# Eight of image 0's lines: depthwise taps moved from VectorE to ScalarE and GpSimd, inside a codebook search

## The chip, the cores and the metric

One core of a Trainium2 chip runs the whole program. The metric is the time of one execution on the device, in microseconds, as the median of several runs. The engines are TensorE (matmuls, into PSUM), VectorE, ScalarE, GpSimd and SyncE; each has its own instruction stream and works through it strictly in order, and they meet only at semaphores. GpSimd also issues the indirect DMAs, the gathers, from its own stream.

## The reference, cut to what matters

Four layers on an input of 2 images of 128 channels and 48 x 48 pixels, each on a group-normed input and added to the running x:

```python
x = x + _L0_conv_ref(_gn(x), ...)     # softmax-weighted dilated branches, 1x1 conv, batch norm
x = x + _L1_conv_ref(_gn(x), codebook)  # nearest of 8192 code vectors for every pixel
x = x + _L2_conv_ref(_gn(x), Wk, bk)    # depthwise 3x3, its weights made from the image
x = x + _L3_conv_ref(_gn(x), ...)     # two deformable 3x3 convolutions with group norms

def _L1_conv_ref(z, codebook):          # per pixel z_flat: argmin over codes
    d = jnp.sum(z_flat ** 2, axis=1, keepdims=True) + jnp.sum(codebook ** 2, axis=1) - 2.0 * jnp.matmul(z_flat, codebook.T)
    idx = jnp.argmin(d, axis=1)
    z_q = codebook[idx].reshape(B, H, W, C)

def _L2_conv_ref(x, Wk, bk):            # nine weights for each channel of each image
    pooled = x.mean(axis=(2, 3))
    kern = jax.nn.relu(pooled @ Wk.T + bk)
    out = lax.conv_general_dilated(xr, kern, ..., feature_group_count=b * c)
```

The change is in the third of them, for image 0.

## The kernel before, in words

Channels lie on the 128 partitions, the 2 x 2304 pixels along the free dimension. The codebook search goes over the pixels in nine blocks of 512 (n = 0 to 8), and for each block over the codebook in four steps (s = 0 to 3) of 16 units (k = 0 to 15). A unit is three bfloat16 matmuls on TensorE (lines 1490 to 1492), which give the scores of 128 blocks of codes for 512 pixels in one of five PSUM buffers, and one running maximum: ScalarE takes units 0 and 1 (line 1667), VectorE scans the other fourteen (line 1962). The maxima are turned by TensorE (line 1379) and copied by ScalarE (line 1601). Then the best block of codes of each pixel is found exactly: for each of the four groups of 128 pixels in a block (u = 0 to 3) VectorE finds the best entry (lines 1777, 1782), GpSimd gathers its eight code vectors (line 2093), multiplies them by the pixel (line 2105), ScalarE sums (line 1592), VectorE chooses among the eight (lines 1788, 1792), GpSimd makes the number of the code (line 2113) and fetches that code's row (line 2118). TensorE turns the four rows (line 1399), VectorE subtracts the pixel from them (line 1807), and GpSimd adds the result to x (lines 2125, 2127). All orders are written out by hand: tables such as `UPPER_AT` say behind which unit an extra piece stands.

Image 0 ends within the fifth block, so its next layer, the depthwise convolution, is done beside the search of the seventh block (n = 6, called L0 in the code). Of image 0's 48 lines VectorE does the upper 24, one instruction per tap on 128 x 1152 elements, that is, multiply by the tap's weight and add into x (`upper_tap`, line 262). TensorE does the lower 24 in three pieces of eight lines, nine diagonal matmuls each (`pe_lower_tap`, line 276), which VectorE adds to x (line 283). At the block's last unit VectorE takes the turned codes, subtracts, and then computes the statistics of all of image 0 (line 139) for the norm ahead of the last layer; the eighth block's scans stand behind this. GpSimd's part of the block's last two steps, in `step` of its program, is: fetch 0, product 3, fetch 1 (s = 2), then fetch 2 and fetch 3 (s = 3), then the add into x. TensorE's turn of the codes stands at the end of step 3 and waits for all four fetches; the eighth block's matmuls are behind it. After the search the four rounds of the deformable convolution follow, for which GpSimd issues some 640 gathers (line 2202).

Of the kernel before, what the change touches and what calls it, by code (L numbers as in the profile page):

```python
# [16 lines left out]
B, H, W = 2, 48, 48  # L17
HW = H * W
N = B * HW
WP = W + 2  # L20
# [4 lines left out]
ROWS = 8  # L25
CH = ROWS * W
NCH = H // ROWS
# [4 lines left out]
TAPS = 9  # L32
# [11 lines left out]
ALU = mybir.AluOpType  # L44
ACT = mybir.ActivationFunctionType
# [147 lines left out]
class Depthwise:  # L193
# [5 lines left out]
    def __init__(self, tools, ctx, a, x, xpad, gm32):  # L199
        self.a, self.x, self.xpad, self.gm32 = a, x, xpad, gm32  # L200
        self.wk = tools.sb(ctx, "wk", [P, TAPS, P])
        self.bk = tools.sb(ctx, "bk", [P, TAPS])
        self.kern = tools.sb(ctx, "kern", [P, TAPS])
        self.pooled = tools.sb(ctx, "pooled", [P, 1])
        self.norm = ImageNorm(tools, ctx)
        self.loaded = tools.sem(ctx, "wk_loaded")
        self.pooled_ready = tools.sem(ctx, "pooled_ready")
        self.kern_ready = tools.sem(ctx, "kern_ready")
        self.applied = tools.sem(ctx, "applied")
        self.done = [tools.sem(ctx, "tap_done") for _ in range(B)]  # L210
        self.kern_done = tools.sem(ctx, "kernels_done")
        self.diag_ready = tools.sem(ctx, "diagonals_ready")
        self.lower_ready = tools.sem(ctx, "lower_taps_ready")
        self.lower_added = tools.sem(ctx, "lower_taps_added")

    def sp(self, sp):
        sp.dma_start(self.wk[:], self.a["wk"]).then_inc(self.loaded, 16)
# [31 lines left out]
    def dve_kernels(self, dve, b, ps):  # L249
# [3 lines left out]
        dve.sem_inc(self.kern_done, 1)  # L253
        dve.wait_ge(self.applied, b + 1)

    def upper_tap(self, dve, k):
        v = self.xpad[:, 0:PADDED].rearrange("p (r w) -> p r w", w=WP)
        v = v[:, k // 3:k // 3 + H // 2, k % 3:k % 3 + W]
        xb = self.x[:, 0, 0:HW // 2].rearrange("p (r w) -> p r w", w=W)
        if k:  # L260
            dve.wait_ge(self.done[0], k)
        dve.scalar_tensor_tensor(xb, v, self.kern[:, k:k + 1], xb, ALU.mult, ALU.add).then_inc(self.done[0], 1)
# [795 lines left out]
def carve(region, sizes):  # L1058

    at, out = 0, []  # L1060
    for n in sizes:
        out.append(region[:, at:at + n])
        at += n
    return out
# [12 lines left out]
def finale(nc, tools, a, code_rows, x, xpad, ident, gm32, gm8, nc2, depthwise, between, places, out):  # L1077
# [42 lines left out]
    L0 = EARLY + 1  # L1120
# [15 lines left out]
    with ExitStack() as ctx:  # L1136
        y0 = tools.sb(ctx, "y_first", [P, HW])
        m0, m1, runs = carve(region_max, [PXT * GROUPS * P] * 2 + [4 * PX])
        maxima = [m.rearrange("p (u g) -> p u g", u=PXT) for m in (m0, m1)]
        r = carve(runs, [PX] * 4)  # L1140
# [79 lines left out]
        off_lead = lead_ps[:, 0:CH]  # L1220
        lower_ps = [off_lead, z_ps.rearrange("p u c -> p (u c)")[:, 0:CH], off_lead]
        diag = region_early[:, PX * EARLY:PX * EARLY + TAPS * P]
        off_ps = [score[0][:, 0:CH]] + [z_ps.rearrange("p u c -> p (u c)")[:, PX - CH:PX]] * (JOBS - 1)
        HALVED = max(BY_SCALAR) + 1
        END_TILES = 2
# [360 lines left out]
        def _(act):  # L1586
# [40 lines left out]
            def lead(n, s, late):  # L1627

                at = n - L0, s, late
                if at == (0, 0, True):  # L1630
                    depthwise.norm.act_root(act, 0)
                if at == (0, 1, False):
                    act.wait_ge(depthwise.norm.affine, 1)
                    act.activation(inner(0), x[:, 0, :].rearrange("p (r w) -> p r w", w=W), ACT.Identity,
                                   bias=depthwise.norm.shift[:], scale=depthwise.norm.scale[:])\
                        .then_inc(depthwise.applied, 1)
                    depthwise.act_diagonals(act, ident, diag)
                if at == (0, 1, True):
                    act.wait_ge(ends_stored, 16 * 2 * JOBS)
                if at == (1, 0, False):  # L1640
                    norm_.act(act, 0)
                    act.activation(y0[:], x[:, 0, :], ACT.Identity, bias=norm_.shift[:], scale=norm_.scale[:])\
                        .then_inc(chunk_ready, NCH)
                if at == (1, 0, True):
                    save_x(0)
                    normalize(0, x[:, 0, :], inner(0), ACT.Identity)
                if at == (1, 1, False):
                    for c in range(1, 5):
                        save_x(c)
                if at == (1, 1, True):  # L1650
                    save_x(5)
                    act.wait_ge(loaded, 16 * len(loads))
                if at == (1, 2, False):
                    save_offsets(0, 0, off_lead)
                if at == (2, 0, True):
                    save_offsets(0, 1, off_lead)
# [112 lines left out]
        def _(dve):  # L1769
# [115 lines left out]
            def lead(n, s, k):  # L1885

                at = n - L0, s, k
                if at == (0, 0, 10):
                    dve.wait_ge(x_added, 1 + 2 * EARLY)
                    depthwise.norm.dve_moments(dve, x[:, 0, :])  # L1890
                if at == (0, 0, 11):
                    depthwise.norm.dve_group(dve, 0, lead_ps[:, 0:ImageNorm.PS])
                if at == (0, 0, 14):
                    depthwise.dve_pool(dve, 0)
                if at == (0, 1, 5):
                    depthwise.dve_kernels(dve, 0, lead_ps)
                unit = (s - 1) * NPR + k
                if n == L0 and unit in UPPER_AT:
                    depthwise.upper_tap(dve, UPPER_AT.index(unit))
                for r, when in enumerate(LOWER_ADDED):  # L1900
                    if n == L0 and unit == when:
                        depthwise.dve_lower_add(dve, r, lower_ps[r])
                if at == (0, 3, 15):
                    dve.wait_ge(depthwise.done[0], TAPS)
                    dve.wait_ge(depthwise.lower_added, NCH // 2)
                    norm_.dve_moments(dve, x[:, 0, :])
                if at == (1, 0, 4):
                    norm_.dve_group(dve, 0, lead_ps[:, 0:ImageNorm.PS])
                if at == (1, 0, 6):
                    norm_.dve_scale(dve, 0)  # L1910
                if at == (1, 2, 5):
                    dve.wait_ge(loaded, 16 * len(loads))
                    prepare(0, 0, "turn")
                if at == (1, 2, 7):
                    place(0, 0, 1)
                if at == (1, 2, 12):
                    weigh(0, 0, 1)
                if at == (2, 1, 3):
                    prepare(0, 1, "turn")
                if at == (2, 1, 7):  # L1920
                    place(0, 1, 1)
                if at == (2, 1, 14):
                    weigh(0, 1, 1)
# [154 lines left out]
        def _(pool):  # L2078
# [68 lines left out]
            def step(n, s):  # L2147
                if not n:
                    return
                if n - 1 in SPILLED and s == 0:  # L2150
                    fetch(n - 1, 3)
                if n in SPILLED:
                    return spilled_step(n, s)
                last = n == NPX - 1
                if last and s == 0:
                    rows(APART, range(5))
                if s == 1:
                    gather(n, 0)
                    if last:
                        apart.wait_ge(score_ready, UNITS - 3 * NPR)  # L2160
                        rows(1, range(2))
                    gather(n, 1)
                    multiply(n, 0)
                    if n - 1 in SPILLED:
                        add(n - 1)
                    multiply(n, 1)
                if s == 2:
                    gather(n, 2)
                    if last:
                        rows(1, range(2, 4))  # L2170
                    multiply(n, 2)
                    gather(n, 3)
                    fetch(n, 0)
                    multiply(n, 3)
                    fetch(n, 1)
                if s == STEPS - 1:
                    fetch(n, 2)
                    fetch(n, 3)
                    if last:
                        rows(APART, range(5, TAPS))  # L2180
                        apart.wait_ge(score_ready, UNITS - 2 * NPR)
                        rows(1, range(4, 8))
                        apart.wait_ge(score_ready, UNITS - NPR)
                        rows(1, range(8, TAPS))
                        rows(3, range(3))
                    else:
                        add(n)
                    if n == NPX - 2:
                        apart.wait_ge(stored, stored_by(0))
                        apart.wait_ge(ends_stored, 16 * 2 * JOBS)  # L2190
                        rows(0)
# [168 lines left out]
```

## Time and profile before

| | us |
|---|---|
| median of 3 runs | 1620.48 (1619.16 to 1622.24) |
| the profiled execution | 1617.55 |
| its span, first to last instruction | 1615.6 |
| TensorE busy | 1201.3 (74%) |
| VectorE busy | 1345.0 (83%) |
| ScalarE busy | 433.0 (27%) |
| GpSimd busy | 1027.3 (64%) |

The chain that ended last is 30% GpSimd (its gathers, above all), 20% TensorE, 13% VectorE and 17% issue, that is, time in which an engine waited for nothing that the profile shows. Busy shares are means over stages of different limits, so they say little about one stage: the search takes roughly the span from 300 to 790 us, the gathers most of the rest. In the rows PE is TensorE, PEld its weight loads, DVE VectorE, ACT ScalarE, POOL GpSimd. TensorE's matmuls are pipelined: one of 512 columns is listed at 0.38 us while the next starts 0.215 us later.

### The profile page before, as it was taken

To read this page: it belongs to the slowest core of one execution; us is meant where nothing else is said; L and a number is where in the kernel's file an instruction comes from. 1 tells how busy PE (TensorE), PEld (TensorE's weight loads), DVE (VectorE), ACT (ScalarE), POOL (GpSimd) and SP (SyncE) were. 2 spreads that over 40 slices of the span, in tenths; PEclk is the share of its full clock that TensorE was granted. 3 is DMA by queue.
4 is the path that set the end of the run, shared out by engine and by line. 5 is a ranking of instruction groups with operands and counts; after the bars stand their busy time and mean duration, and the time that the engine had idled before them with its cause. 6 is when DMAs were issued, how large, how long until landed. Compare 5 with 4: busy or idle time off the path is not lost.

```text
span 1615.6 us, 19850 instructions
## 1 busy us (share of the span) xinstructions
PE 1201.3 (74%) x6050; PEld 750.2 (46%) x6094; DVE 1345.0 (83%) x1880; ACT 433.0 (27%) x1363; POOL 1027.3 (64%) x983
## 2 busy tenths in 40 slices
PE   5898999699999999888755776676655566545565
PEld 2454555344444445443344554454444344434454
DVE  5678899789999999888859889997788777887776
ACT  1241000214444334343366221221212212111112
POOL 5169799613444433247677677777777777777773
PEclk9889999899999999999978887797777777767667
DMA  4041000011212111055566797787877878777774
GB/s 166 19 150 61 1 0 0 15 45 47 58 45 57 47 33 41 22 173 150 162 208 196 226 282 209 210 270 229 249 211 229 249 230 250 209 232 209 212 210 146
DMA packets 111102, 232.65 MB, mean 144 GB/s; under 512 B 14676, under 2 KB 60500, under 8 KB 110748
## 3 DMA queue, kind: packets, MB, share of 16 engines
q0 software_dynamic: 58176, 191.30, 40.3%
q1 hardware_dynamic: 52828, 40.17, 7.9%
q8 instruction: 47, 0.77, 0.2%
q14 instruction: 51, 0.42, 0.1%
HBM read 205.15 MB, written 26.26 MB: 143 GB/s over the span
## 4 chain that ended last, share of the span: by engine, by line
POOL 30%; PE 20%; issue 17%; DVE 13%; DMA 1%; ACT 1%; DVEq 0%; POOLq 0%; ACTq 0%
POOL code_region L2202 12%; POOL max_region L2202 6%; POOL late_region L2202 6%; POOL early_region L2202 5%; DVE max_region L1962 4%; PE score L1492 3%; PE score L1490 3%; PE score L1491 2%; PE lead_score L1491 2%; PE lead_score L1490 2%; PE lead_score L1492 2%; PE score L1531 1%; DVE lead_score L293 1%; DVE best L1777 1%; PE turn_ps L1379 1%
## 5 line engine op out<-in xcount | busy, mean ns | idle before, releaser
L2202 POOL DMA_INDIRECT code_region<-corners,lead_region x252 | 242.3, 961 | 77.8 <-issue 75.2
L1962 DVE SCALAR_TENSOR_TENSOR max_region<-score,nc,max_region 128x512 f32<-128x512 f32 x324 | 233.2, 745 | 25.2 <-PE score L1492 22.8
L775 POOL TENSOR_TENSOR prod_acc<-prod_acc,prod_pool 128x768 f32<-128x768 f32 (+8 forms) x118 | 171.9, 1456 | 61.1 <-DVE prod_pool L750 52.5
L1531 PE MATMUL score<-ident,code_region 128*128 128x128 f32 x540 | 97.2, 341 | 79.9 <-DVE code_region L2015 74.0
L2202 POOL DMA_INDIRECT early_region<-corners,lead_region x136 | 128.7, 946 | 41.3 <-issue 41.1
L2202 POOL DMA_INDIRECT max_region<-corners,lead_region x130 | 123.9, 953 | 41.3 <-issue 38.4
L2202 POOL DMA_INDIRECT late_region<-corners,lead_region x126 | 119.4, 948 | 43.2 <-issue 38.1
L1962 DVE SCALAR_TENSOR_TENSOR max_region<-lead_score,nc,max_region 128x512 f32<-128x512 f32 x180 | 133.1, 745 | 9.9 <-PE lead_score L1492 9.2
L2093 POOL DMA_INDIRECT late_region<-code_rows,block_id x35 | 35.7, 1020 | 142.2 <-DVE block_id L1782 72.1
L1531 PEld LDWEIGHTS score<-ident,code_region 128*128 128x128 f32 x540 | 79.1, 177 | 97.6 <-DVE code_region L2015 90.0
L2011 DVE TENSOR_TENSOR lead_score<-lead_score,code_region 128x768 f32<-128x768 f32 x78 | 75.4, 966 | 39.5 <-DMA code_region<-corners,lead_region 36.4
L750 DVE TENSOR_TENSOR prod_pool<-spread,xpad 128x768 f32<-128x768 f32 (+8 forms) x118 | 90.3, 791 | 3.5 <-PE spread L673 3.0
L1601 ACT COPY max_region<-turn_ps 128x512 f32<-128x512 f32 x72 | 42.1, 585 | 187.3 <-PE turn_ps L1379 187.3
L695 PE MATMUL y_ps<-prod_pe,w_scale 128*128 128x96 f32 (+7 forms) x360 | 89.3, 371 | 0.0
L1592 ACT ACTIVATE late_region<-late_region 128x129 f32<-128x129 f32 x280 | 82.6, 299 | 23.0 <-POOL late_region L2105 15.6
L2105 POOL TENSOR_TENSOR late_region<-late_region 128x1032 f32<-128x1032 f32 x32 | 71.0, 2219 | 23.4 <-DMA late_region<-code_rows,block_id 22.5
L1717 ACT COPY code_region<-score 128x384 f32<-128x384 f32 x72 | 34.3, 477 | 177.2 <-PE score L1531 171.6
L673 PE MATMUL spread<-wta,sel_a 108*128 x352 | 74.7, 315 | 7.2 <-DVE prod_pool L750 3.2
L1531 PE MATMUL score<-ident,early_region 128*128 128x128 f32 x310 | 50.2, 318 | 38.8 <-DVE early_region L2015 29.7
L750 DVE TENSOR_TENSOR prod_pe<-spread,xpad 128x752 f32<-128x752 f32 (+7 forms) x92 | 56.9, 630 | 24.6 <-PE spread L673 24.1
L2015 DVE TENSOR_TENSOR code_region<-lead_score,code_region 128x768 f32<-128x768 f32 x78 | 74.7, 957 | 2.7
L1509 PE MATMUL turn_ps<-code_region,max_region 128*128 128x256 f32 x216 | 71.8, 483 | 4.9 <-ACT code_region L1717 4.9
(298 smaller groups left out, 3080.7 us busy)
## 6 DMA issues: line engine op xcount, KB each, us to landing
corners<-lead_region SPq DMA_DIRECT2D x72, 192.0 KB, 4.5
corners<-lead_region SPq DMA_DIRECT2D x8, 576.0 KB, 6.7
code_rows<-codes_n SPq DMA_DIRECT2D x8, 516.0 KB, 3.9
codes_t<-in_codes_t SPq DMA_DIRECT2D x8, 512.0 KB, 3.6
codes_n<-in_codes SPq DMA_DIRECT2D x8, 512.0 KB, 4.1
code_region<-corners,lead_region POOLq DMA_INDIRECT x252, 3.7
x<-in_x SPq DMA_DIRECT2D x2, 1152.0 KB, 6.5
out<-x SPq DMA_DIRECT2D x4, 576.0 KB, 3.9
```

The lines of the kernel that those rows point to most:

```text
L673: mm = pe.matmul(to, sel[:, kk, :], v, start=True, stop=True)
L695: mm = pe.matmul(dst, w_scale[:, o["i"] + 1, :], src.rearrange("p (r w) -> p r w", r=rows), start=False, stop=last, skip_group_check=True)
L750: dve.tensor_tensor(to, w, v, ALU.mult).then_inc(prod_ready, 1)
L775: pool.tensor_tensor(to, to, v, ALU.add).then_inc(pooled, 1)
L1490: pe.matmul(o, ch[g][:, w], high, start=True, stop=False)
L1492: pe.matmul(o, cl[g][:, w], high, start=False, stop=True).then_inc(score_ready, 1)
L1531: mm = pe.matmul(tps[g][:, k * P:(k + 1) * P], quad(T, 3 * g + k)[:, c * P:(c + 1) * P], ident, start=c == low, stop=c == CORNERS - 1, is_ ...
L1592: act.activation(v, v, ACT.Identity, accum_out=fine[:, u, j:j + 1]).then_inc(summed, 1)
L1962: dve.scalar_tensor_tensor(r, score[SLOT[k]], nc2[:, m:m + 1], r, ALU.add, ALU.max).then_inc(dve_took, 1)
L2011: return dve.tensor_tensor(upper_ps, bc(w[:, k, 0:2], P), q[:, k, 0:2], ALU.mult)
L2015: dve.tensor_tensor(q[:, k, 2:4], upper_ps, q[:, k, 2:4], ALU.add).then_inc(halved, 1)
L2202: pool.indirect_dma_start(quad(T, k), None, table[j].rearrange("n s c -> n (s c)"), bass.IndirectOffsetOnAxis(index[j % B][:, at:at + 1], 0))\
```

## The change

Of VectorE's 24 lines the last eight (lines 16 to 23, 384 elements, called the middle lines) go to two other engines. For each of the nine taps ScalarE multiplies the shifted lines by the tap's weight into one of six buffers, carved from `y0`, which is free at this time; GpSimd adds the buffer into x. Five taps stand in step 2 and four in step 3 of the seventh block, on both engines. A piece on ScalarE from the seventh on waits until its buffer's add is done, each add waits for its piece and for the add before it, and VectorE waits for all nine adds ahead of image 0's statistics. TensorE's program is the same.

```diff
+    def act_middle_tap(self, act, k, to, held):
+        if k >= held:
+            act.wait_ge(self.middle_added, k - held + 1)
+        at = (NCH // 2 - 1) * (ROWS * WP) + k // 3 * WP + k % 3
+        v = self.xpad[:, at:at + ROWS * WP].rearrange("p (r w) -> p r w", w=WP)[:, :, 0:W]
+        act.activation(to.rearrange("p (r w) -> p r w", w=W), v, ACT.Identity,
+                       scale=self.kern[:, k:k + 1]).then_inc(self.middle_weighted, 1)
+
+    def pool_middle_tap(self, pool, k, v):
+        xc = self.x[:, 0, (NCH // 2 - 1) * CH:NCH // 2 * CH]
+        pool.wait_ge(self.middle_weighted, k + 1)
+        if k:
+            pool.wait_ge(self.middle_added, k)
+        pool.tensor_tensor(xc, xc, v, ALU.add).then_inc(self.middle_added, 1)
+
     def upper_tap(self, dve, k):
+        lines = (NCH // 2 - 1) * ROWS
...
-        v = v[:, k // 3:k // 3 + H // 2, k % 3:k % 3 + W]
-        xb = self.x[:, 0, 0:HW // 2].rearrange("p (r w) -> p r w", w=W)
+        v = v[:, k // 3:k // 3 + lines, k % 3:k % 3 + W]
+        xb = self.x[:, 0, 0:lines * W].rearrange("p (r w) -> p r w", w=W)
...
+        weighted_lines = carve(y0[:], [CH] * NCH)
...
+                if at in ((0, 2, True), (0, 3, False)):
+                    for t in range(5) if s == 2 else range(5, TAPS):
+                        depthwise.act_middle_tap(act, t, weighted_lines[t % NCH], NCH)
...
                     dve.wait_ge(depthwise.lower_added, NCH // 2)
+                    dve.wait_ge(depthwise.middle_added, TAPS)
                     norm_.dve_moments(dve, x[:, 0, :])
...
                     fetch(n, 1)
+                    if n == L0:
+                        for t in range(5):
+                            depthwise.pool_middle_tap(pool, t, weighted_lines[t % NCH])
                 if s == STEPS - 1:
                     fetch(n, 2)
+                    if n == L0:
+                        for t in range(5, TAPS):
+                            depthwise.pool_middle_tap(pool, t, weighted_lines[t % NCH])
                     fetch(n, 3)
```

GpSimd's instructions from the third product of the seventh block to the add into x, before (`late_region` holds candidates, fetched rows and the difference, `code` the numbers of the codes):

```order
L2113 TENSOR_TENSOR code<-block_code,fine_id 128x1
L2118 DMA late_region<-in_codes,code 128x128
L2105 TENSOR_TENSOR late_region<-late_region 128x1032
L2113 TENSOR_TENSOR code<-block_code,fine_id 128x1
L2118 DMA late_region<-in_codes,code 128x128
L2113 TENSOR_TENSOR code<-block_code,fine_id 128x1
L2118 DMA late_region<-in_codes,code 128x128
L2113 TENSOR_TENSOR code<-block_code,fine_id 128x1
L2118 DMA late_region<-in_codes,code 128x128
L2125 TENSOR_TENSOR late_region<-late_region 128x512
```

and in the changed program, where the adds into x read `y_first`, the six buffers:

```order
L2136 TENSOR_TENSOR code<-block_code,fine_id 128x1
L2141 DMA late_region<-in_codes,code 128x128
L2128 TENSOR_TENSOR late_region<-late_region 128x1032
L2136 TENSOR_TENSOR code<-block_code,fine_id 128x1
L2141 DMA late_region<-in_codes,code 128x128
L271 TENSOR_TENSOR x<-x,y_first 128x384 x5
L2136 TENSOR_TENSOR code<-block_code,fine_id 128x1
L2141 DMA late_region<-in_codes,code 128x128
L271 TENSOR_TENSOR x<-x,y_first 128x384 x4
L2136 TENSOR_TENSOR code<-block_code,fine_id 128x1
L2141 DMA late_region<-in_codes,code 128x128
L2148 TENSOR_TENSOR late_region<-late_region 128x512
```

Five adds now stand ahead of the third fetch and four more ahead of the fourth.

ScalarE's instructions in the block's last two steps, before (the copies out of `turn_ps` hand on the turned maxima, the groups of eight are the sums of products):

```order
L1592 ACTIVATE late_region,fine<-late_region 128x129 x8
L1667 ACTIVATE max_region<-lead_score,nc_35 128x512 x2
L1592 ACTIVATE late_region,fine<-late_region 128x129 x8
L1601 COPY max_region<-turn_ps 128x4x128 x2
L1667 ACTIVATE max_region<-lead_score,nc_35 128x512 x2
```

and in the changed program:

```order
L1611 ACTIVATE late_region,fine<-late_region 128x129 x8
L263 ACTIVATE y_first<-xpad,kern 128x384 x5
L1689 ACTIVATE max_region<-lead_score,nc_37 128x512 x2
L1611 ACTIVATE late_region,fine<-late_region 128x129 x8
L263 ACTIVATE y_first<-xpad,kern 128x384 x4
L1620 COPY max_region<-turn_ps 128x4x128 x2
L1689 ACTIVATE max_region<-lead_score,nc_37 128x512 x2
```

Five pieces now stand ahead of step 3's two activations of scores, and four ahead of the copies of the turned maxima.

## Rows read from the trace of the kernel before

**Rows 1.** Chain of waits from 560 to 800 us: start us, us, what.

```profile
658.18 0.65 PE lead_score L276 x2
...
661.48 2.54 DMA late_region<-in_codes,code
...
665.37 2.86 DVE n_stats L139 x6
```

**Rows 2.** TensorE's busy time in stretches: stretch, length, busy (count), granted clock, DMA.

```profile
618.70:663.00 44.30, 44.09 (x184) 1.00 0.10 29
678.00:680.00 2.00, 2.00 (x9) 0.50 0.00 0
```

**Rows 3.** Groups by line from 618.69 to 663 us: count, busy us, mean ns, idle.

```profile
L262 DVE SCALAR_TENSOR_TENSOR x<-xpad,kern,x 128x1152 f32<-128x1152 f32 x9 | 13.2, 1467 | 0.0
```

**Rows 4.** TensorE's timeline at the block's end: start us, us, instruction [idle before <-releaser].

```profile
662.77 0.38 PE L1492 MATMUL score<-code_region 128*128 128x512 bf16 x1
664.07 0.66 PE L1399 MATMUL z_ps<-ident,late_region 128*128 128x128 f32 x4 [0.92 <-DMA late_region<-in_codes,code]
...
669.03 0.35 PE L149 MATMUL lead_score<-n_mean_var,gm 128*128 128x2 f32 x2 [1.72 <-DVEq L144]
```

**Rows 5.** GpSimd's timeline from 646 to 665 us.

```profile
649.10 2.85 POOL L2105 TENSOR_TENSOR late_region<-late_region 128x1032 f32<-128x1032 f32 x1 [0.42 <-DMA late_region<-code_rows,block_id]
...
652.90 0.98 POOL L2118 DMA_INDIRECT late_region<-in_codes,code  x1 [0.81 <-POOL code L2113]
...
655.37 0.96 POOL L2118 DMA_INDIRECT late_region<-in_codes,code  x1 [0.81 <-POOL code L2113]
660.49 0.19 POOL L2113 TENSOR_TENSOR code<-block_code,fine_id 128x1 uint32<-128x1 uint32 x1 [4.16 <-DVE fine_id L1792]
661.48 0.96 POOL L2118 DMA_INDIRECT late_region<-in_codes,code  x1 [0.81 <-POOL code L2113]
```

**Rows 6.** Timelines of GpSimd (first row) and VectorE: a product, three taps, a scan.

```profile
636.68 2.20 POOL L2105 TENSOR_TENSOR late_region<-late_region 128x1032 f32<-128x1032 f32 x1 [3.24 <-DMA late_region<-code_rows,block_id]
...
638.13 1.97 DVE L262 SCALAR_TENSOR_TENSOR x<-xpad,kern,x 128x1152 f32<-128x1152 f32 x1
...
648.48 1.41 DVE L262 SCALAR_TENSOR_TENSOR x<-xpad,kern,x 128x1152 f32<-128x1152 f32 x1
...
654.43 0.74 DVE L1962 SCALAR_TENSOR_TENSOR max_region<-lead_score,nc,max_region 128x512 f32<-128x512 f32 x1
...
657.17 1.41 DVE L262 SCALAR_TENSOR_TENSOR x<-xpad,kern,x 128x1152 f32<-128x1152 f32 x1
```

**Rows 7.** ScalarE's timeline: the places of the pieces, and an activation from SBUF.

```profile
646.85 1.27 ACT L1667 ACTIVATE max_region<-lead_score,nc 128x512 f32<-128x512 f32 x2 [2.95 <-PE lead_score L1492]
...
656.92 0.58 ACT L1601 COPY max_region<-turn_ps 128x512 f32<-128x512 f32 x1 [2.49 <-PE turn_ps L1379]
659.95 0.58 ACT L1601 COPY max_region<-turn_ps 128x512 f32<-128x512 f32 x1 [2.44 <-PE turn_ps L1379]
...
680.99 2.59 ACT L1615 ACTIVATE xpad<-x,n_shift,n_scale 128x1152 f32<-128x1152 f32 x2
```

**Rows 8.** GpSimd's timeline: an add of 384 elements and its successor, two dependent adds.

```profile
101.94 0.99 POOL L775 TENSOR_TENSOR prod_acc<-prod_acc,prod_pool 128x384 f32<-128x384 f32 x1 [0.17 <-DVE prod_pool L750]
...
103.01 2.58 POOL L775 TENSOR_TENSOR prod_acc<-prod_acc,prod_pool 128x672 f32<-128x672 f32 x2
...
665.53 1.27 POOL L2125 TENSOR_TENSOR late_region<-late_region 128x512 f32<-128x512 f32 x1 [3.09 <-DVE late_region L1807]
666.89 1.26 POOL L2127 TENSOR_TENSOR x<-x,late_region 128x512 f32<-128x512 f32 x1
```

**Rows 9.** TensorE's timeline after a wait.

```profile
677.16 0.64 PE L1379 MATMUL turn_ps<-ident,max_region 128*128 128x128 f32 x4 [2.14 <-DVE max_region L1962]
...
678.88 1.06 PE L1387 MATMUL z_ps<-ident,late_region 128*128 128x128 f32 x4
```

**Rows 10.** GpSimd's timeline: the first gather of the long run.

```profile
733.89 0.96 POOL L2202 DMA_INDIRECT early_region<-corners,lead_region  x1
```

More of the change, by code:

```diff
@@ L214, in __init__ @@
         self.lower_added = tools.sem(ctx, "lower_taps_added")
+        self.middle_weighted = tools.sem(ctx, "middle_lines_weighted")
+        self.middle_added = tools.sem(ctx, "middle_lines_added")
     def sp(self, sp):
```

## The prediction

> **What bounds the kernel now.** I read the chain of waits first, then TensorE's busy share over the stretch of the seventh pixel block, then the four engines' timelines there, and last what follows the block. The chain [rows 1] shows that the stretch is on the path to the end: it runs along TensorE's depthwise matmuls (line 276) up to 658 us, then through a gather that lands in 2.54 us, and on to VectorE's statistics of image 0. Within the stretch, from 618.70 to 663.00 us, TensorE is busy 44.09 of 44.30 us at the full clock [rows 2]. The reader is to see that nothing that VectorE does can make this stretch shorter: TensorE has no gap in which it waits for VectorE. VectorE's nine taps fill 13.2 us of the same stretch [rows 3], but they fill VectorE, not the path.
>
> At the end of the stretch the chain changes hands. TensorE's last score matmul starts at 662.77, and the next thing it does is to turn the fetched code rows at 664.07, after 0.92 us without work, waiting for the gather [rows 4]. That gather is the fourth of the block's code fetches, which GpSimd issues at 661.48; the third was issued at 655.37, and between them GpSimd waited 4.16 us for VectorE's index [rows 5]. So GpSimd's program order is 0.92 us from being the bound of the block, and there is about 4 us of room on GpSimd ahead of the last fetch. This is the place that decides.
>
> **The change, part by part.**
>
> VectorE loses a third of each tap. One tap of 1152 elements takes 1.41 us and a scan of 512 elements 0.74 [rows 6], so 384 elements cost (1.41 - 0.74) x 384/640 = 0.40 us and nine taps give back 3.6 us to VectorE. What hid behind it is TensorE, which goes on without a gap [rows 2]; VectorE only waits longer for scores. Worth on the path: nothing, or at the very most the 0.92 us.
>
> ScalarE gets nine activations of 384 elements. Two of 1152 take 2.59 us together [rows 7], so a third of one is 0.43 and I take 0.5. Five stand ahead of the activations at 646.85, where ScalarE had been idle for 2.95 us, and four ahead of the copy at 656.92, where it had been idle for 2.49 us [rows 7]. 2.5 us and 2.0 us fit. With six buffers the last piece has to wait until the third add is done; by the times below that is 656.8, so the copy comes about 0.4 us late. The copy after it, at 659.95, waited 2.44 us for TensorE [rows 7], so this is swallowed. If the adds were slower by half, TensorE's second turn would be late too. I cost ScalarE at nothing.
>
> GpSimd gets nine adds of 384 elements, five between the second and third fetch and four between the third and fourth. In the branches stage an add of just this size has 0.99 us in its row and the next add starts 1.07 us after it; adds of 512 elements that depend on one another, as these do, start 1.36 us apart [rows 8]. I take 1.07 for the size, keep 0.99 and 1.36 as the ends, and so get 9 x 1.07 = 9.6 us where 4.16 us are free.
>
> In order of time: the second fetch ends at 652.90 + 0.98 = 653.88 [rows 5]. The product ahead of it took 2.85 us there against 2.20 us for the same product earlier [rows 5, 6], because a tap of VectorE was in its way; taps are shorter and earlier now, so I take off half of the 0.65 us and start the adds at 653.6. Five adds end at 658.95. VectorE's last tap comes at 657.17 [rows 6], will take 1.41 - 0.40 = 1.0 us and meets one of them: 0 to 1 us, I take 0.4, so 659.35; the tap before it may add as much. Code number and wait are 0.99 us, as from 660.49 to 661.48, and issuing 0.98 [rows 5]: the third fetch is off at 661.3. Four more adds end at 665.6, the code number and its wait at 666.6. That is 666.6 - 661.48 = 5.1 us later than now for the fourth fetch. VectorE's index, which ended its wait at 660.49, is there by then whatever GpSimd does. From the issue to TensorE's turn nothing changes (2.59 us [rows 4, 5]), so the turn comes at 669.2.
>
> The meeting of a tap and a GpSimd instruction is shown by one pair: a product on GpSimd from 636.68 to 638.88, and a tap that starts at 638.13 and takes 1.97 us instead of 1.41 [rows 6]: it ends as if it had begun at 638.7. The Trainium skill (SBUF — State Buffer, SBUF: two separate sides) has a rule that speaks against putting these adds beside these taps: VectorE with two SBUF inputs and GpSimd share a port pair which whoever comes first keeps for the whole instruction. By that rule the trace agrees, for the tap gets going about when the product ends; every meeting would cost the later of the two what is left of the other, and the sum would be 5.5 us or up to 1.6 more; if both ran side by side it would be 0.4 less.
>
> The added wait on VectorE (for all nine adds, ahead of image 0's statistics) costs nothing by itself: it stands behind the subtraction that needs the turned codes at 669.2, and the ninth add is done at 665.6. Behind both are queued VectorE's statistics, and behind these the scans of the eighth block.
>
> TensorE now idles from 663.0 to 669.2 instead of 1.1 us. After an idle time of 2.14 us at 677.16 its granted clock was 0.50, the lower of its two levels, from 678 to 680, and a group of four turns took 1.06 us, where it takes 0.66 at the full clock [rows 2, 4, 9]. So I add 0.4 us for the turn of the codes. The score matmuls behind it are hidden: VectorE has some 4 us of subtraction and statistics before it wants them, as the next TensorE work that it releases starts at 669.03 [rows 4]. The ends are 0 and 1.5 us. The Trainium skill (TensorE: Matmul & The Clock Gate, What's actually happening) says the same, that an idle TensorE drops to 1.2 GHz; by it the slow turn is certain and the sum stays as it is.
>
> Nothing later takes this back. GpSimd's sum into x after the eighth block ends just ahead of the first long run of gathers at 733.89 [rows 10], so GpSimd's stream of gathers, which is 30% of the chain, starts later by the same amount.
>
> Sum: 5.1 + 0.4 = 5.5 us. The profiled execution took 1617.55 us (its span 1615.6 and 1.95 around it), so 1623.05 against itself; the median of the runs is 1620.48, and I forecast 1620.5 + 5.5 = **1626.0 us**. The ends of the prices: adds at 0.99 take off 0.7 us and at 1.36 add 2.6; the start of the adds 0.3 either way; the taps from 0.4 less to 1.6 more; the clock 0.4 less to 1.1 more. That is 3.7 to 11.1 us in all, 4 to 8 as the likely part: 1624.5 to 1628.5.
>
> **The rivals.**
>
> The adds hide and nothing changes. To be done when the fourth index is there at 660.5 the nine would have to take (4.16 + 0.65)/9 = 0.53 us each, half of what the row of this size shows [rows 8]. Then the path goes along TensorE as before: 1619.6 to 1621. For it: spans on GpSimd are rough. Chance 0.08.
>
> VectorE is the bound after all. If TensorE was waiting for freed score buffers in gaps that the records do not show, the 3.6 us would be gained: 1620.5 - 3.6 = 1616.9. It decides only if the adds hide as well, since a late fourth fetch holds TensorE in any case. For it: VectorE is dense, too. Against it: TensorE's 44.09 of 44.30 us [rows 2], and matmuls evenly spaced. Chance 0.04.
>
> The adds are slow and the ring of buffers bites. At 1.36 us each the fourth fetch is 7.7 us late; with both taps in the way and ScalarE's last pieces waiting for buffers, so that its copies hold TensorE's second turn, 9 to 10 us: about 1630. For it: the same port is wanted by taps and adds. Against it: only two taps are left when the adds start. Chance 0.13.
>
> **How the numbers follow.** The forecast has 0.75. A difference under 0.2% (3.2 us) is about what a measurement of this kernel can't tell from none. Slower by more: nearly all of the forecast and all of the slow case, 0.88. Within: the hidden case and a rest of the forecast, 0.08. Faster: 0.04. The range reaches down into the hidden case's side to 1622.5 and up to the slow case's time, 1630.5.
>
> **What would show it.** GpSimd's timeline has nine adds of 384 elements, about 1.07 us apart, and the fourth fetch some 5 us after the fourth index is there, with no wait for VectorE before it. TensorE has a gap of about 6 us ahead of its turn of the codes, blamed on that gather, and then a few us at a clock of 0.5. VectorE's taps take about 1.0 us, its waits for scores within the stretch grow by about 3.6 us in all, and TensorE's 44 us stay as they are. The prediction is wrong if TensorE's stretch gets shorter, if the adds take about 0.5 us, or if the fourth fetch is no later against the last score matmul than now.

## The result, and the profile after

The change makes the kernel slower: 1623.3 us (median of 19 runs) against 1618.5 us for the kernel before (19 runs), a ratio of 1.0033 with the interval 1.0022 to 1.0045. On 1618.5 us that is 5.3 us, with 3.6 to 7.3 us as its interval; the two medians lie 4.8 us apart; the forecast was 5.5 us. The profiled execution of the changed kernel took 1624.45 us, its span 1622.4 us.

In the trace after, everything is already 1.22 us later where the seventh block's stretch starts (TensorE's first depthwise matmul starts at 619.91 us, before at 618.69), ahead of any edited instruction. To compare an event with its time in the kernel before, take 1.22 us off.

GpSimd's timeline after, in the same columns as [rows 5]: start us, us, instruction, idle time before it and what ended it.

```profile
649.13 2.20 POOL L2128 TENSOR_TENSOR late_region<-late_region 128x1032 f32<-128x1032 f32 x1 [0.86 <-DMA late_region<-code_rows,block_id]
...
652.29 0.98 POOL L2141 DMA_INDIRECT late_region<-in_codes,code  x1 [0.81 <-POOL code L2136]
653.29 6.96 POOL L271 TENSOR_TENSOR x<-x,y_first 128x384 f32<-128x384 f32 x5
660.22 0.18 POOL L2136 TENSOR_TENSOR code<-block_code,fine_id 128x1 uint32<-128x1 uint32 x1
661.21 0.96 POOL L2141 DMA_INDIRECT late_region<-in_codes,code  x1 [0.81 <-POOL code L2136]
662.18 4.43 POOL L271 TENSOR_TENSOR x<-x,y_first 128x384 f32<-128x384 f32 x4
666.57 0.19 POOL L2136 TENSOR_TENSOR code<-block_code,fine_id 128x1 uint32<-128x1 uint32 x1
667.57 0.96 POOL L2141 DMA_INDIRECT late_region<-in_codes,code  x1 [0.81 <-POOL code L2136]
```

The reader is to see two things. The code number at 666.57 has no wait for VectorE before it, where the one of before waited 4.16 us [rows 5]: GpSimd comes to it late by itself. And the fourth fetch is issued at 667.57, which is 666.35 on the clock of before, 4.87 us later than at 661.48.

TensorE's timeline at the end of the block, as in [rows 4]:

```profile
663.99 0.38 PE L1511 MATMUL score<-code_region 128*128 128x512 bf16 x1
670.06 1.12 PE L1418 MATMUL z_ps<-ident,late_region 128*128 128x128 f32 x4 [5.70 <-DMA late_region<-in_codes,code]
```

The last score matmul comes exactly when it came before (662.77 + 1.22), and the gap behind it has grown from 0.92 to 5.70 us, ended by the same gather. The turn takes 1.12 us instead of 0.66.

TensorE in stretches, as in [rows 2]: stretch, length, busy (count), granted clock, DMA share, GB/s.

```profile
619.90:664.20 44.30, 44.29 (x188) 1.00 0.11 29
664.20:670.00 5.80, 0.17 (x1) 0.83 0.04 11
670.00:672.00 2.00, 1.94 (x7) 0.50 0.00 0
672.00:674.00 2.00, 2.00 (x7) 0.50 0.00 0
674.00:676.00 2.00, 2.00 (x10) 0.80 0.00 0
```

The stretch itself is as full as before and as long. After the idle time the granted clock is at 0.50, the lower of its levels, until about 674 us.

VectorE's timeline shows where the loss reaches the path: the subtraction waits for the turn, and image 0's statistics start behind it with no wait of their own.

```profile
671.22 0.69 DVE L1829 TENSOR_TENSOR late_region<-z_ps,late_region 128x512 f32<-128x512 f32 x1 [5.56 <-PE z_ps L1418]
671.83 2.85 DVE L139 BATCH_NORM_STATS2 n_stats<-x 128x6 f32<-128x384 f32 x6
```

Groups by line on VectorE from 619.9 to 664.2 us, as in [rows 3], and two of its waits in the stretch, after and then before (engine, line, what it waited for: us in total, times, longest):

```profile
L280 DVE SCALAR_TENSOR_TENSOR x<-xpad,kern,x 128x768 f32<-128x768 f32 x9 | 9.4, 1045 | 0.0
```

```profile
DVE max_region L1985 <- PE lead_score L1511: 3.3, 7, 0.8
...
DVE max_region L1985 <- PE score L1511: 3.0, 3, 1.6
```

```profile
DVE max_region L1962 <- PE score L1492: 1.8, 2, 1.6
DVE max_region L1962 <- PE lead_score L1492: 1.6, 3, 0.8
```

The taps gave back 13.2 - 9.4 = 3.8 us. Most of it, 2.9 us, VectorE spent waiting for scores: 6.3 us of waits, where the same two rows of before read 3.4 us.

ScalarE's timeline, with its pieces (line 263) and the work behind them:

```profile
645.03 2.62 ACT L263 ACTIVATE y_first<-xpad,kern 128x384 f32<-128x384 f32 x5
648.07 1.28 ACT L1689 ACTIVATE max_region<-lead_score,nc 128x512 f32<-128x512 f32 x2 [0.41 <-PE lead_score L1511]
...
653.73 1.22 ACT L263 ACTIVATE y_first<-xpad,kern 128x384 f32<-128x384 f32 x2
656.02 0.61 ACT L263 ACTIVATE y_first<-xpad,kern 128x384 f32<-128x384 f32 x1 [1.07 <-POOL x L271]
657.17 0.62 ACT L263 ACTIVATE y_first<-xpad,kern 128x384 f32<-128x384 f32 x1 [0.54 <-POOL x L271]
658.14 0.59 ACT L1620 COPY max_region<-turn_ps 128x512 f32<-128x512 f32 x1 [0.36 <-PE turn_ps L1398]
```

Both copies and activations still wait for TensorE after the pieces, so nothing on ScalarE has become late. They come at the times of [rows 7] plus 1.22.

### The profile page after: what moved, and what is told of

Read it like the earlier page. It is cut to its first block and busy times, and to the rows that moved or that the text cites. A ratio compares the mean times of both kernels' runs of the same rounds, so it can differ in the third digit from the quotient of the medians.

```text
span 1622.4 us, 19920 instructions
## 1 busy us (share of the span) xinstructions
PE 1211.0 (75%) x6094; PEld 754.8 (47%) x6094; DVE 1343.4 (83%) x1880; ACT 438.0 (27%) x1372; POOL 1037.0 (64%) x992
```

## Experiments

Each kernel was timed in five rounds beside the kernel before: the first four on one chip (before: 1617.13 us), the last three on another (before: 1617.56 us). Diffs are against the changed kernel. The verdicts go by the ratio to the kernel before and its 95% interval in brackets; the ratio is not the quotient of the two medians, and one thousandth of it is 1.6 us.

The theory (A in the expectations): the loss is GpSimd's program order, nine adds ahead of the fourth fetch, and VectorE's relief is worth nothing. The rivals: the relief is worth something that the adds eat up (B); the adds and VectorE's taps hold one another up wherever they stand (C); the added wait ahead of the statistics costs time by itself.

**The relief alone (relief_only).** VectorE's taps cover 16 lines, and the kernel leaves out the sums of the middle eight.

```diff
-                    for t in range(5) if s == 2 else range(5, TAPS):
-                        depthwise.act_middle_tap(act, t, weighted_lines[t % NCH], NCH)
...
-                    dve.wait_ge(depthwise.middle_added, TAPS)
...
-                            depthwise.pool_middle_tap(pool, t, weighted_lines[t % NCH])
```

> VectorE's taps cover 16 lines and nobody does the middle eight (their depthwise sum is left out), so there are no pieces and no adds. Theory A (the cost is GpSimd's order: nine adds ahead of the fourth code fetch; VectorE's relief is worth nothing because TensorE bounds the stretch): 0 to 0.9 us under the kernel before, and the TensorE stretch of 44.3 us unchanged. Rival B (VectorE bounds the stretch and its relief pays): 3.6 us under the kernel before. Rival C (the cost is adds and taps meeting at a shared port): as A here.

Measured: 1619.26 us, ratio 0.9998 (0.9982 to 1.0014). From the stretch's first matmul at 616.82 to the turn it is 45.34 us, before 45.38. The rows of TensorE's turn, and of GpSimd's code numbers ahead of the third and the fourth fetch:

```profile
662.16 0.66 PE L1418 MATMUL z_ps<-ident,late_region 128*128 128x128 f32 x4 [0.88 <-DMA late_region<-in_codes,code]
```

```profile
651.15 0.88 POOL L2132 TENSOR_TENSOR code<-block_code,fine_id 128x1 uint32<-128x1 uint32 x1 [0.96 <-DVE fine_id L1811]
...
658.62 0.19 POOL L2132 TENSOR_TENSOR code<-block_code,fine_id 128x1 uint32<-128x1 uint32 x1 [4.83 <-DVE fine_id L1811]
```

GpSimd's wait for the fourth index ends 41.80 us after the first matmul, exactly as in before. So without adds the 3.8 us that VectorE gives back are worth nothing on the path. The rows also give the room that the shorter taps leave on GpSimd between the second and the fourth fetch: 0.96 and 4.83 us of waits and 0.69 us by which the first code number is longer than the second, 6.48 us together. The change puts nine adds there that take 6.96 + 4.43 = 11.39 us. What does not fit is 4.91 us, and its fourth fetch is 4.87 us late.

**The adds alone (adds_only).** VectorE keeps its 24 lines; the pieces go into a ring of five buffers, and the adds into a sixth whose sum nobody uses.

```diff
-    def pool_middle_tap(self, pool, k, v):
-        xc = self.x[:, 0, (NCH // 2 - 1) * CH:NCH // 2 * CH]
+    def pool_middle_tap(self, pool, k, v, xc):
...
-        pool.tensor_tensor(xc, xc, v, ALU.add).then_inc(self.middle_added, 1)
+        pool.tensor_tensor(xc, xc if k else v, v, ALU.add).then_inc(self.middle_added, 1)
...
-        lines = (NCH // 2 - 1) * ROWS
+        lines = H // 2
...
-                            depthwise.pool_middle_tap(pool, t, weighted_lines[t % NCH])
+                            depthwise.pool_middle_tap(pool, t, weighted_lines[t % 5], weighted_lines[5])
```

> VectorE keeps all 24 lines, and the pieces and adds run at the places of the change, but into a spare buffer with five pieces in the ring. The output is the reference's. A: as slow as the change, 4 to 6.5 us over the kernel before, with TensorE's gap of 5 to 7 us ahead of the turn of the codes. B: the change less its relief, that is 4.8 + 3.6 = 8.4 us over. C: more than the change, since taps of 1.4 us meet the adds, 6 to 8 us over.

Measured: 1623.8 us, ratio 1.0037 (1.002 to 1.0053), that is 6.0 us over (3.2 to 8.6): not to be told from the whole change, but no timing that tells A from B or C. TensorE's two turns and GpSimd's third product and fourth fetch in this kernel:

```profile
657.93 0.63 PE L1397 MATMUL turn_ps<-ident,max_region 128*128 128x128 f32 x4 [1.32 <-ACT max_region L1619]
...
667.65 1.12 PE L1417 MATMUL z_ps<-ident,late_region 128*128 128x128 f32 x4 [5.86 <-DMA late_region<-in_codes,code]
```

```profile
646.19 2.84 POOL L2127 TENSOR_TENSOR late_region<-late_region 128x1032 f32<-128x1032 f32 x1 [0.42 <-DMA late_region<-code_rows,block_id]
...
665.11 0.96 POOL L2140 DMA_INDIRECT late_region<-in_codes,code  x1 [0.81 <-POOL code L2135]
```

The adds alone bring a gap as long as the change's (5.70 us) with VectorE's work as it was, so the cost comes from the adds. The delay is longer, though. The fourth fetch comes 49.22 us after the stretch's first matmul at 615.89, in the change 47.66 and in before 42.79; the gap is hardly longer than the change's because TensorE has lost 1.32 us before it, on ScalarE, whose pieces wait for the five buffers. The adds take as long as in the change but start 1.7 us later: the third product starts 1.1 us later and takes 2.84 us instead of 2.20, as in before. So with the adds in the way VectorE's relief is worth some 1.6 us after all, not through VectorE's own work but because shorter taps let GpSimd come to the adds sooner.

**The adds behind the fourth fetch (adds_late).** ScalarE's last four pieces move with them, behind its copies of the turned maxima.

```diff
-                if at in ((0, 2, True), (0, 3, False)):
+                if at in ((0, 2, True), (0, 3, True)):
...
-                    if n == L0:
-                        for t in range(5):
-                            depthwise.pool_middle_tap(pool, t, weighted_lines[t % NCH])
...
+                    fetch(n, 3)
                     if n == L0:
-                        for t in range(5, TAPS):
+                        for t in range(TAPS):
                             depthwise.pool_middle_tap(pool, t, weighted_lines[t % NCH])
-                    fetch(n, 3)
```

> All nine adds stand behind the fourth fetch, and ScalarE's last four pieces behind its copies. A: the fourth fetch is on time and TensorE's gap ahead of the turn is 0.9 us as before; but VectorE's statistics now wait for the ninth add, done some 9.7 us after the fetch is issued, at 672 of the old time instead of 665.4: 6 to 8 us over the kernel before, by another wait. C: the adds meet no tap, so under the change, 1 to 3 us over.

Measured: 1625.25 us, ratio 1.0042 (1.0026 to 1.0059). The fetch and the turn are on time again (659.03 and 661.57, 42.80 and 45.34 us after the stretch's first matmul); the timelines of TensorE, GpSimd and VectorE, one row each:

```profile
661.57 0.66 PE L1418 MATMUL z_ps<-ident,late_region 128*128 128x128 f32 x4 [0.88 <-DMA late_region<-in_codes,code]
...
660.01 10.13 POOL L271 TENSOR_TENSOR x<-x,y_first 128x384 f32<-128x384 f32 x9
...
670.27 2.86 DVE L139 BATCH_NORM_STATS2 n_stats<-x 128x6 f32<-128x384 f32 x6 [7.31 <-POOL x L271]
```

Now the added wait is the one that ends last: 7.31 us for the nine adds. That is 6.8 us over the kernel before (4.2 to 9.5). So that wait is free in the change only because the late turn hides it, and moving adds behind the fetch moves the cost rather than removes it.

**The adds early (adds_early).** Five adds stand behind the block's second product, four behind the third gather of rows, where GpSimd waits for other engines; ScalarE's pieces move one step forward. ScalarE's edit, then GpSimd's:

```diff
-                if at in ((0, 2, True), (0, 3, False)):
-                    for t in range(5) if s == 2 else range(5, TAPS):
+                if at in ((0, 1, True), (0, 2, False)):
+                    for t in range(5) if s == 1 else range(5, TAPS):
...
                     multiply(n, 1)
+                    if n == L0:
+                        for t in range(5):
+                            depthwise.pool_middle_tap(pool, t, weighted_lines[t % NCH])
                 if s == 2:
                     gather(n, 2)
+                    if n == L0:
+                        for t in range(5, TAPS):
+                            depthwise.pool_middle_tap(pool, t, weighted_lines[t % NCH])
```

> Five adds stand behind the second product (step 1) and four behind the third gather (step 2), where GpSimd waits 9.7 and 3.2 us for ScalarE and a gather; the pieces on ScalarE go one step earlier, too. A: nothing is left ahead of the fetches, so 0.9 us under to 0.5 us over the kernel before. B: 3.6 us under. C: adds now meet four or five taps, so still 2 to 4 us over.

Measured: 1617.8 us, ratio 0.9996 (0.9978 to 1.0013): the time of before, with all of the change's work done. GpSimd's timeline:

```profile
625.46 4.97 POOL L271 TENSOR_TENSOR x<-x,y_first 128x384 f32<-128x384 f32 x4 [4.04 <-ACT y_first L263]
630.88 1.85 POOL L271 TENSOR_TENSOR x<-x,y_first 128x384 f32<-128x384 f32 x1 [0.45 <-POOL x L271]
...
635.13 4.97 POOL L271 TENSOR_TENSOR x<-x,y_first 128x384 f32<-128x384 f32 x4
...
660.39 0.19 POOL L2136 TENSOR_TENSOR code<-block_code,fine_id 128x1 uint32<-128x1 uint32 x1 [4.83 <-DVE fine_id L1814]
661.38 0.96 POOL L2141 DMA_INDIRECT late_region<-in_codes,code  x1 [0.81 <-POOL code L2136]
```

Adds and taps meet more here than in the change (three adds take 1.5 us or more instead of two, and the nine taps 10.3 us instead of 9.4), and still GpSimd waits 4.83 us for VectorE ahead of the fourth fetch, and the turn comes 45.37 us after the stretch's first matmul. Meetings of adds and taps alone are not what makes the change slow; the place is.

**Four adds in the free time (four_between).** Five adds early, as in adds_early, and four where the change has them, between the third and fourth fetch. ScalarE's edit:

```diff
-                if at in ((0, 2, True), (0, 3, False)):
-                    for t in range(5) if s == 2 else range(5, TAPS):
+                if at in ((0, 1, True), (0, 3, False)):
+                    for t in range(5) if s == 1 else range(5, TAPS):
```

> As adds_early, but the last four adds stand where the change has them, between the third and the fourth fetch. Theory A (room: only what goes beyond the 4.2 us for which GpSimd waits there costs time): four adds of 1.07 us fill that room, so 0.9 us under to 1.0 us over the kernel before, with TensorE's gap ahead of the turn at 0.9 to 1.5 us. Rival C (any add between the fetches costs its time): 4 x 1.07 = 4.3 us over.

Measured: 1617.23 us, ratio 1.0001 (0.9984 to 1.0018). GpSimd and TensorE:

```profile
653.69 4.98 POOL L271 TENSOR_TENSOR x<-x,y_first 128x384 f32<-128x384 f32 x4
658.63 0.19 POOL L2136 TENSOR_TENSOR code<-block_code,fine_id 128x1 uint32<-128x1 uint32 x1
659.62 0.96 POOL L2141 DMA_INDIRECT late_region<-in_codes,code  x1 [0.81 <-POOL code L2136]
...
662.16 0.66 PE L1418 MATMUL z_ps<-ident,late_region 128*128 128x128 f32 x4 [1.01 <-DMA late_region<-in_codes,code]
```

Four adds fill the 4.83 us that adds_early leaves there, no wait for VectorE is left, and TensorE's gap is 1.01 us. That is the free time of the argument measured from its other side: what the change puts there beyond that time is what costs.

**Relieving TensorE instead (pe_relief).** With the adds early, ScalarE and GpSimd take a third of TensorE's lines (40 to 47), and VectorE has its 24 again.

```diff
-        at = (NCH // 2 - 1) * (ROWS * WP) + k // 3 * WP + k % 3
+        at = (NCH - 1) * (ROWS * WP) + k // 3 * WP + k % 3
...
-    LOWER_AT = [9 + 4 * i // 3 for i in range(NCH // 2 * TAPS)]
-    LOWER_ADDED = 22, 34, 45
+    LOWER_AT = [9 + 2 * i for i in range(2 * TAPS)]
+    LOWER_ADDED = 28, 45
```

> The adds early, and the eight lines taken from TensorE (its third piece, lines 40 to 47) instead of VectorE, which keeps 24. A (TensorE bounds the stretch): TensorE's stretch loses nine taps of 0.645 us, 5.8 us, and VectorE, which waited 3.4 us in it, becomes the bound: 2 to 3.5 us under the kernel before. Rival B (VectorE bounds the stretch already): no change, or 0.5 us under for the one sum into x that VectorE loses.

Measured: 1615.99 us, ratio 0.9994 (0.998 to 1.0007): 1.0 us under, not to be told from before, and short of the 2 to 3.5 us that A expected; by its time alone B's "no change" would stand as well. The trace shows that TensorE was the bound, but by little: the turn comes 43.95 us after the first matmul at 614.25, 1.4 us earlier than in before. VectorE takes over: it is busy 41.62 of 43.45 us, and it ends GpSimd's wait for the last index. TensorE's turn, and GpSimd ahead of it:

```profile
658.20 0.66 PE L1418 MATMUL z_ps<-ident,late_region 128*128 128x128 f32 x4 [2.59 <-DMA late_region<-in_codes,code]
```

```profile
643.58 3.46 POOL L2126 TENSOR_TENSOR late_region<-late_region 128x1032 f32<-128x1032 f32 x1 [0.27 <-DMA late_region<-code_rows,block_id]
...
648.00 2.00 POOL L2139 DMA_INDIRECT late_region<-in_codes,code  x1 [0.81 <-POOL code L2134]
...
654.72 0.19 POOL L2134 TENSOR_TENSOR code<-block_code,fine_id 128x1 uint32<-128x1 uint32 x1 [2.74 <-DVE fine_id L1812]
```

A product of 3.46 us instead of 2.20 and an issue of 2.00 instead of 0.98 show meetings with taps again.

**Thirds for three (three_way).** ScalarE and GpSimd take lines 20 to 31, VectorE has 20 and TensorE 16.

```diff
-        at = (NCH // 2 - 1) * (ROWS * WP) + k // 3 * WP + k % 3
+        at = (H // 2 - 4) * WP + k // 3 * WP + k % 3
...
-        lines = (NCH // 2 - 1) * ROWS
+        lines = H // 2 - 4
```

> As pe_relief, but ScalarE and GpSimd take twelve lines (20 to 31), VectorE keeps 20 and TensorE 16; four pieces of 576 elements in the ring. A: TensorE's stretch 5.8 us shorter and VectorE's work 9 x 0.2 + 0.5 us less, so 3.5 to 5.8 us under the kernel before, unless the longer adds (1.4 us each, 12.8 us where GpSimd has 9.7 and then 9 us of room) push the later fetches. B: 2.3 us under.

Measured: 1616.54 us, ratio 0.9996 (0.9982 to 1.0009), a miss: 0.6 us under (2.9 under to 1.5 over), where 2.3 or more were expected. From the first matmul at 620.50 to the turn at 664.89 it is 44.39 us. The adds of 576 elements hold GpSimd for so long that its third product starts at 652.54:

```profile
626.89 7.63 POOL L271 TENSOR_TENSOR x<-x,y_first 128x576 f32<-128x576 f32 x4 [3.49 <-ACT y_first L263]
...
636.70 8.36 POOL L271 TENSOR_TENSOR x<-x,y_first 128x576 f32<-128x576 f32 x5
```

ScalarE's sums, which need GpSimd's products, waited 10.4 us for them, where they waited 3.9 us in before. That this is what took the gain is argued from these rows; no run varied it. No split that was tried beats the kernel before by more than its interval.

## Why the prediction was right, step by step

- *The place that decides.* Right, but not as worded. GpSimd is not "0.92 us from being the bound": that gap of TensorE was already ended by the gather, whose fetch waits for VectorE's index. What an add between the fetches has to fit into is GpSimd's wait for that index.
- *VectorE's relief is worth nothing.* Right for the path along TensorE: relief_only has the time of before, and the waits for scores grew by 2.9 us (forecast 3.6). It is worth some 1.6 us to GpSimd once the adds stand ahead of the fetch, as adds_only shows; the forecast had 0.3 us of it.
- *ScalarE is hidden.* Right. A piece takes 0.60 us and the next starts 0.5 us after it, the value taken. Two pieces waited for a buffer (1.07 and 0.54 us); the copy behind them still waited for TensorE, so it was not even 0.4 us late.
- *The adds start at 653.6.* They start at 652.07 on the clock of before, 1.5 us earlier. The product took 2.20 us, so the whole 0.65 us went and not half of it; it also started earlier by 1.2 us. GpSimd's instructions ahead of it were held less: the issue of the block's third gather of rows took 1.58 us instead of 1.98, and the instruction on `block_code` behind the fourth 0.35 instead of 0.74. The same three are at 1.57, 0.34 and 2.19 us in relief_only, and at 1.97, 0.74 and 2.84 in adds_only with its full taps, so it is the shorter taps that do this.
- *Five adds and a tap end 5.75 us later.* They took 6.96 us. The row of after that has them hides this in a sum; apart, the median add takes 1.0 us, the second 1.54 and the last 1.82. Both stand where VectorE's taps run:

```profile
654.07 1.05 DVE L280 SCALAR_TENSOR_TENSOR x<-xpad,kern,x 128x768 f32<-128x768 f32 x1
...
658.39 1.01 DVE L280 SCALAR_TENSOR_TENSOR x<-xpad,kern,x 128x768 f32<-128x768 f32 x1
```

```profile
654.45 1.54 POOL L271 TENSOR_TENSOR x<-x,y_first 128x384 f32<-128x384 f32 x1
...
658.43 1.82 POOL L271 TENSOR_TENSOR x<-x,y_first 128x384 f32<-128x384 f32 x1
```

  The add at 658.43 ends at 660.25, as if it had begun at about 659.25, and the tap beside it ends at 659.40. Two meetings cost 0.55 + 0.83 us; the forecast had 0.4 for one and said that the other "may add as much". So two terms were mis-sized, the adds by 1.2 us and their start by 1.5 us, and that they cancel is luck: the mechanism was right, and the sum is closer than its terms. The Trainium skill (SBUF — State Buffer, SBUF: two separate sides) has the rule for such a meeting, one engine keeping the shared port pair for a whole instruction; by that rule the trace agrees, on GpSimd's side as well as on VectorE's.
- *Four more adds, then the fourth fetch, 5.1 us late.* 4.43 us against 4.28, and 4.87 us late in all.
- *A slow clock adds 0.4 us.* The turn took 1.12 us instead of 0.66, at a granted clock of 0.50. With it VectorE's subtraction is 5.24 us late (671.22 - 1.22 against 664.76 in the kernel before); the forecast had 5.5. The score matmuls at the low clock up to 674 us were hidden, as the statistics of 2.85 us and what hangs on them come first.
- *Nothing later takes it back.* Not quite what the two traces show: from the subtraction to the first gather of the long run [rows 10] it is 69.13 us before (733.89 - 664.76) and 68.08 after (739.30 - 671.22), so 4.19 us of the delay arrive there. What differs lies at the place of [rows 9]. After the same idle time of 2.14 us the clock is not down in the trace after, and the group of four turns takes 0.60 us instead of 1.06:

```profile
683.61 0.63 PE L1398 MATMUL turn_ps<-ident,max_region 128*128 128x128 f32 x4 [2.14 <-DVE max_region L1985]
...
684.73 0.60 PE L1406 MATMUL z_ps<-ident,late_region 128*128 128x128 f32 x4
```

  This is not the change's doing, or not alone: adds_early, four_between and pe_relief, which have no late fetch, keep the full clock there too after the same 2.14 us, and relief_only and three_way fall to 0.50 like the kernel before. Against the two that kept it with the change's work, adds_early and four_between, from the stretch's first matmul to the first gather the change has 119.39 us and they have 114.44 and 114.42: 4.95 us, like against like.

The forecast's 1626.0 us lies 2.7 us over the median; 2.0 of these are the median of the kernel before, which was 1620.48 us over the three runs known then and 1618.5 us over 19.

Still open: why the clock falls after the idle time at [rows 9] in some traces and not in others was not tried.

## What to carry to other kernels

Before giving an engine more work, read how long it waits ahead of each DMA that it issues: here nine adds of some 11 us in all were free in one place of GpSimd's program and cost 5.3 us in another, some 26 us later. Relief for an engine that is busy but waits for another (VectorE for TensorE's scores) comes out as longer waits, and the row that tells this is the other engine's busy share of the stretch; it can still pay elsewhere, here by holding GpSimd less. Moving a late instruction past the critical issue helps only if nobody waits for its result right behind it.

## What the runs showed of the hardware

Dependent adds of 384 elements on GpSimd take 1.00 us and start 1.15 us apart where no tap runs (four in 4.43 us). One that meets a tap takes longer: 1.85 us for one that starts with a tap of 1.00 us (adds_early, 630.88), and 2.25 us for one that starts with a tap of 1.40 us (pe_relief, 626.30). Small instructions are held as well: a GpSimd instruction on 128x1 elements, 0.21 us where it meets nothing, took 1.49 us in pe_relief, from 629.79 us on, where a tap of VectorE ran from 629.80 for 1.39 us. Indirect issues are held too: 2.00 us instead of 0.98 in pe_relief, at 648.00, where a tap ran from 647.75 for 1.39 us. After idle times of the same 2.14 us TensorE's granted clock fell to 0.50 in three traces (before, relief_only, three_way) and stayed at 1.00 in four (after, adds_early, four_between, pe_relief).
